# A selective-scan mixer on one core: other states turned on TensorE, and a table of steps for the rest of the chunk

## The reference

```python
xz = xseq @ in_proj_w.T
xin, z = jnp.split(xz, 2, axis=-1)
...                                   # causal convolution of 3 taps over tokens
u = silu(conv(xin) + conv_b)
dbc = u @ x_proj_w.T                  # dt (24 columns), B (16), C (16)
dt = softplus(dt @ dt_proj_w.T + dt_proj_b)
A = -exp(A_log)
def step(h, inp):
    dA = exp(dt_t[..., None] * A)
    h = dA * h + (dt_t * u_t)[..., None] * B_t[:, None, :]
    y = einsum('bdn,bn->bd', h, C_t)
...
y = (y + u * D) * silu(z)
return y @ out_proj_w.T
```

## Time and profile before

| | |
|---|---|
| median of 3 runs (lowest, highest) | 3687.34 us (3685.7, 3687.74) |
| the profiled execution | 3684.98 us, of which the span 3683.2 us |
| busy over the span | DVE 3306.3 us, 90%; PE 3295.5, 89%; ACT 2742.8, 74%; POOL 2574.8, 70% |
| TensorE clock granted, mean | 0.963 |
| DMA | 253.99 MB, mean 69 GB/s |

### The profile page before, as it was taken

How to read it: one execution, slowest core, us unless ns; L and a number is a source line. 1 busy time by engine, 2 the same in 40 slices (tenths; PEclk the granted TensorE clock), 3 DMA queues, 4 the chain that set the end, 5 groups by cost and what they waited for, 6 DMA issues and landing times. The chain is left out here.

```text
span 3683.2 us, 48473 instructions
## 1 busy us (share of the span) xinstructions
PE 3295.5 (89%) x16194; PEld 2284.1 (62%) x16194; DVE 3306.3 (90%) x3472; ACT 2742.8 (74%) x5286; POOL 2574.8 (70%) x2045
## 2 busy tenths in 40 slices
PE   5989989898988989898999989898789998889997
PEld 2655656566566666566565666566557776557776
DVE  3999999999999999999999999999967887876886
ACT  5987797787879778877977787788655554876553
POOL 3898988989898988989898998989931111561100
PEclk7999999999999999999999999999999999999998
DMA  4020211202020211202020211202120113650112
GB/s 137 10 95 19 95 47 58 87 18 87 19 95 19 95 61 44 87 19 89 16 104 21 84 67 38 87 19 94 53 61 35 53 53 141 237 191 32 70 36 87
DMA packets 81532, 253.99 MB, mean 69 GB/s; under 512 B 15212, under 2 KB 24044, under 8 KB 71044
## 3 DMA queue, kind: packets, MB, share of 16 engines
q1 hardware_dynamic: 80516, 249.84, 18.8%
q10 hardware_dynamic: 768, 1.05, 0.1%
HBM read 208.93 MB, written 41.95 MB: 68 GB/s over the span
## 5 line engine op out<-in xcount | busy, mean ns | idle before, releaser
L956 POOL TENSOR_TENSOR slot<-dtu,b_rep 128x512 f32<-128x512 f32 x1056 | 1330.0, 1279 | 231.2 <-PE ysum L454 230.5
L454 PE MATMUL ysum<-ident,slot 128*128 128x128 f32 x6144 | 847.8, 283 | 128.6 <-DVE slot L1065 82.7
L454 PEld LDWEIGHTS ysum<-ident,slot 128*128 128x128 f32 x6144 | 728.4, 146 | 360.4 <-issue 235.0
L754 ACT ACTIVATE state<-dt,aneg 128x512 f32<-128x512 f32 x1056 | 718.4, 688 | 219.7 <-DVE slot L1065 195.4
L966 POOL TENSOR_TENSOR slot<-slot,c_rep 128x512 f32<-128x512 f32 x672 | 851.6, 1279 | 16.2 <-DVE slot L1057 8.4
L1065 DVE TENSOR_TENSOR slot<-state,c_rep 128x512 f32<-128x512 f32 x864 | 578.8, 671 | 0.0
L1057 DVE TENSOR_TENSOR_SCAN slot<-state,slot 128x512 f32<-128x512 f32 x288 | 343.5, 1207 | 25.4 <-ACT state L754 22.5
L1057 DVE TENSOR_TENSOR_SCAN slot<-state,carry,slot 128x512 f32<-128x512 f32 x288 | 361.0, 1268 | 2.3 <-POOL slot L956 1.2
L745 ACT ACTIVATE slot<-dt,aneg 128x512 f32<-128x512 f32 x480 | 333.6, 709 | 7.2 <-PE ysum L454 7.2
L572 PE MATMUL state<-diag_b,dtu_t 128*128 128x128 f32 x2304 | 313.3, 280 | 14.0 <-issue 11.4
L1616 ACT ACTIVATE hid<-ph_l,bias_l 128x512 f32<-128x512 f32 x240 | 165.0, 691 | 204.6 <-PE ph_l L1427 203.3
(11 more groups left out here) (272 smaller groups left out, 6174.0 us busy)
## 6 DMA issues: line engine op xcount, KB each, us to landing
c_rep<-rows_of_b_and_c SPq DMA_DIRECT2D x64, 1024.0 KB, 4.7
xres_l<-between_layers SPq DMA_DIRECT2D x18, 1536.0 KB, 9.9
b_rep<-rows_of_b_and_c SPq DMA_DIRECT2D x32, 768.0 KB, 4.1
xn_l<-between_layers SPq DMA_DIRECT2D x13, 1536.0 KB, 7.4
b_rep<-rows_of_b_and_c SPq DMA_DIRECT2D x16, 1024.0 KB, 4.8
between_layers<-y SPq DMA_DIRECT2D x10, 1536.0 KB, 6.4
xn<-in_x SPq DMA_DIRECT2D x16, 768.0 KB, 4.5
xres<-in_x SPq DMA_DIRECT2D x16, 768.0 KB, 4.5
```

The source lines that it names most:

```text
L454: last = mm(ysum[:, cols], slot[:, (NS * k + n) % SLOTS, cols], ident[:], start=first and j == 0, stop=final, is_transpose=True, skip_grou ...
L754: af(state[:, (NS * k + n) % BANKS], dt[:, k], ACT.Exp, scale=aneg[:, k, n:n + 1]).then_inc(exp_done, 1)
L956: tt(slot[:, q % SLOTS], dtu[:, k % 2], b_rep[:, b_row(n)], ALU.mult).then_inc(dbu_done, 1)
```

## The change

Only constants of the tables change. State 14 is turned in place of 13, so 13 gets a diagonal matrix. Sums, turns of y and u, gatings, residual copies, the mean and centring, gate and in projections, convolution parts, the dt of all blocks, the product dt u on POOL, the turn of B and the diagonal matrices get other steps.

```diff
-PE_N, TURN_N, SCALE_AHEAD, SCALED = (7, 11, 13, 14, 15), (11, 13), 6, 2
-SUM_AT = (6, 7, 7, 3, 8, 10, 10, 10, 12, 15, 15, 11, 14, 15, 15, 15)
-
-COPY_Y, TURN_Y_AT, GATED_Y_AT = 5, (27, 35, 51, 74, 81, 1), (32, 40, 55, 76, 84, 1)
+PE_N, TURN_N, SCALE_AHEAD, SCALED = (7, 11, 13, 14, 15), (11, 14), 6, 2
+SUM_AT = (4, 7, 7, 3, 8, 10, 11, 11, 14, 13, 15, 15, 15, 14, 15, 16)
+
+COPY_Y, TURN_Y_AT, GATED_Y_AT = 5, (27, 35, 52, 74, 81, 1), (29, 40, 55, 76, 84, 0)
...
-OUT_AT, OUT_PER = (0, 1, 9), (3, 1, 1)
-OUT_IN, RES_AT = (BX, BY, BX), (9, 16, 19)
+OUT_AT, OUT_PER = (0, 1, 8), (3, 1, 1)
+OUT_IN, RES_AT = (BX, BY, BX), (10, 16, 20)
...
-MEAN_AT, CENTER_AT, SQUARE_AT, VAR_AT, RSTD_AT, SCALE_AT = 15, 22, 26, 23, 30, 28
-GATE_AT, GATE_IN = (20, 22, 35, 49, 64, 70), (BX, BZ, BY, BX, BY, BZ)
-IN_AT, IN_IN = (30, 32, 33, 35, 45, 47), (BY, BZ, BX, BX, BY, BZ)
-CONV_IN_AT, CONV_AT = (34, 37, 39, 48, 49, 53), (35, 36, 37, 49, 51, 52)
+MEAN_AT, CENTER_AT, SQUARE_AT, VAR_AT, RSTD_AT, SCALE_AT = 18, 21, 26, 23, 30, 28
+GATE_AT, GATE_IN = (20, 21, 34, 50, 64, 70), (BX, BZ, BY, BX, BY, BZ)
+IN_AT, IN_IN = (28, 32, 33, 36, 45, 48), (BY, BZ, BX, BX, BY, BZ)
+CONV_IN_AT, CONV_AT = (34, 37, 38, 45, 50, 54), (33, 35, 37, 49, 51, 52)
...
-XP_AT, XP_COPY_AT = 51, 59
-DT_AT, DT_IN = (56, 57, 63, 70, 2, 18), (BX, BY, BZ, BX, BZ, BZ)
-DT_READ_AT = (61, 63, 73, 77, 8, 23)
-DT_ADD_AT = (66, 75, 81, 95, 10, 40)
+XP_AT, XP_COPY_AT = 52, 59
+DT_AT, DT_IN = (55, 58, 62, 68, 3, 18), (BX, BY, BZ, BX, BZ, BZ)
+DT_READ_AT = (61, 64, 73, 78, 9, 23)
+DT_ADD_AT = (68, 73, 82, 95, 14, 33)
 EARLY = 4
-DT_U_AT = 4
-TURN_U_AT, COPY_U_AT = (90, 9, 30, 39, 60, 75), (95, 18, 34, 47, 64, 85)
-TURN_B_AT, COPY_B_AT = 84, 92
-DIAG_AT = (94, 94, 0, 15, 5)
+DT_U_AT = 1
+TURN_U_AT, COPY_U_AT = (88, 6, 28, 39, 57, 77), (95, 17, 32, 48, 65, 82)
+TURN_B_AT, COPY_B_AT = 83, 91
+DIAG_AT = (94, 90, 0, 4, 6)
```

## The result

The change is slower, by a quarter of a per cent: 3695.62 us median of 13 runs (3690.25 to 3700.78), against 3685.43 (3684.35 to 3687.74) for the kernel before on the same chip, ratio 1.0025, 95% interval [1.0018, 1.0033]. I had forecast 3671, within 3657 to 3686: both the time and its sign were wrong. The profiled execution took 3695.98 us (span 3694.2), that of before 3684.98 (3683.2).

A forecast was written before the change was run, and what follows sets the result against it. PE was taken to bound a chunk's start and DVE its end. Seven even chunks 2.3 us shorter, seven odd 0.3 longer, plus first and last chunks: 16 us less, 3669; forecast 3671 against the median, range 3657 to 3686.

The forecast's parts named there:

- first five steps: Chunk start to block 1: gating and dt_proj 4 win 0.3 us, state 11 loses 0.2 to 0.4, state 29 comes 1.17 earlier (even chunks).
- the 1.63 us called issue: PE's idle before state 14's product in even chunks, taken as waiting for ACT's diagonal matrix; it would go.
- the second rival: Before state 14's product, PE's 1.63 us idle is truly issue and stays: total gain about 5 us, 3682; chance 0.08.
- the rival on the slower side: At PE's step 6, turn_u 1 blocks PE until ACT has read dt 4: 21 us more at 2.5 us blocking, 3709; chance 0.14.
- item 6: Late in even chunks: waits of 0.54, 0.30 and 0.39 us go, state 75's 0.48 stays; 1.1 to 1.2 us won.
- state 75's 0.48: Block 4, n 11, even chunk: DVE's 0.48 us wait stays, as gate_proj 5 waits for ACT's read of dt 2.
- Item 7: Sum 8 two steps later delays POOL's drive of n 4 about 1.6 us; costs nothing, with 1.3 us in hand.
- rival of the clock: At gate_proj 5, the lower clock reaches nine more middle chunks: 14 us back, 3685, no change; chance 0.14.
- item 5: Block 1, state 29 (n 13): 1.17 us earlier in even chunks; at most 0.46 later in odd ones, 0.3 taken.
- same chance: At gate_proj 5, the lower clock may instead leave the five chunks that have it: 8 us less, 3663.

## Why the prediction was wrong

**Its first five steps hold.** The wait for y is 2.38 (forecast 2.4), none at state 7, 1.10 at state 11 (about 1), 0.20 at state 15 (0.3 or less), 0.98 at state 29 (about 1). State 29's scan starts at +48.39 in place of +49.75, 1.36 earlier where I took 1.17. PE has no idle before state 13's product or 14's turn, so the 1.63 us called issue were ACT's matrix; the second rival falls, and both kernels without the exchange show the gap. turn_u 1 waits for nothing, so the rival on the slower side that I priced, 3709, did not happen.

**The step that failed is item 6, late in the chunk.** Item 6 found the waits that go (0.54, 0.30 and 0.39 did go) and held that state 75's 0.48 stays and nothing else comes. It had no term for dt_proj 1, which the change moves behind drive 62, and so put it at nothing. (Item 7 does not name it either; the cover that item 7 prices held, as state 20 does not wait.) In the trace of before, drive 63 ended 0.5 us ahead of its scan, and since dt_proj 1 is ahead of drive 63 in both rows I took its move for nothing. What was missing is that drive 62 cannot move up into the place that the product leaves, because it waits for ACT's copy of the carry. So a product taken from in front of that wait leaves PE idle and comes back behind it at full price: 0.98 us of idle, 0.74 of waiting at state 63. That DVE comes 1.4 us earlier by the gains that I had myself summed is not needed for it: the kernel before with this entry alone has 0.97 us of idle and 0.72 of waiting. By itself that is 5.9 us; with the clock's drops that came with it, the entry cost 27, where the whole forecast was a gain of 16.

**The rival of the clock had the size and not the place.** I gave it 0.14 and 14 us, at gate_proj 5 in nine more chunks. It came at +110 and +115 with the sums and drive 63, and went on into gate_proj 5 in three more chunks: together with state 63's own 10.8 us, less what POOL takes back, it took 27. I called it chance ("nothing makes it systematic"). It is systematic in that a table entry changes the pattern in chunk after chunk and in most runs: with dt_proj 1 at 57 five runs lie within 2.1 us, in the change thirteen lie within 10.5, most at 3695.5 to 3696.2 and the others near 3691 and 3701. It is not certain in every run, though: with the gating moved too, three of eleven lie at 3681 to 3687.

**The sum's total came out, its parts did not.** With dt_proj 1 at 57 the profiled execution is 16.1 us below that of before; the forecast said 16. But that is two things. Where the clock disturbs neither kernel, an even chunk went from 164.5 to 162.8 us and an odd one from 164.5 to 164.9: 7 x (1.7 - 0.4) = 9 us, where I had 7 x (2.3 - 0.3) = 14. The odd chunks' loss is the forecast's. In the even ones item 5 gave its share (1.36), and only 0.3 is left for item 6, in place of 1.15: its three waits went, but DVE now waits 8.5 us in 21 times for POOL's drives, mostly at states 73, 74 and 89, which the table's other moves probably bring about (no run took them back). The other 7 to 8 us are the five state-75 waits of 2 us, which go too: the "same chance" that the clock's rival mentioned (8 us less). That the total is right to the tenth is luck. The exchange of states has no value of its own either: it is 46 us less in the new table and 6 more in the old one.

What stays open is what in PE's work lets the clock fall at one place and not at another. With a spare product in the 0.98 us of idle at +107 the drops at +110 and +115 are gone. But the same idle stands in chunks 2, 6, 10 and 14 of the change and, with 0.97 us, in every even chunk of the kernel before with dt_proj 1 at 58, and there no drop follows it for 17 us or more; 2.36 us at +111 do no harm; and the two dt products both put back give a worse pattern. So the amount of idle time at one place is not the rule. That the time follows the entry dt_proj 1 is shown in both kernels; by which way the entry moves the drops is not. By the Trainium skill (TensorE: Matmul & The Clock Gate, Part 1, A second HAM failure mode) one kernel whose TensorE idled briefly and often between groups of matmuls had its clock swing between the two levels. The 0.98 and 1.96 us ahead of the drops agree; the 2.36, and the 0.98 of chunks 2, 6, 10 and 14, do not.

## What to carry to other kernels

When a product is moved behind an instruction that waits for another engine, it can cost its whole length and save nothing: look for what the waiting instruction waits for, and price the product at the place where the wait ends, with the consumer as early as the rest of the change makes it. In a kernel where TensorE is some 90% busy, look at where the granted clock falls in each chunk, not only at its mean: here one product moved by one step, with the drops that came with it, turned a saving of 18 us into a loss of 10. A table tuned entry by entry holds together as a whole, so test a change by putting single entries back; one of some sixty decided this one.

## What was not expected of the hardware

- More work made the kernel faster: 15 further products of 1.05 us, one in each chunk's gap, took 22 us off.
- The time on the lower clock level does not rank kernels: 92.2 us at 3695.3 us, 93.8 at 3668.9, 129.7 at 3685.4 (before), 157.0 at 3679.4. What stands there counts: before and in the change a drop inside gate_proj 5 makes state 75 wait 2.0 to 2.5 us, and one over the five sums costs 1.57 at state 70 when it starts at +115.6 and nothing at +117.5.
- The pattern of drops locks to the chunks, with a period of two (dt_proj 1 at 57: +137 and +151 in even chunks, +118 in odd ones) or of four (the change: +110, +127, +141, +154 in one, +115, +129, +143 in the next, then +138, +151 and +139), and can change within an execution, as in the run with the spare product.
